# A two-layer attention and FFN kernel: the norm of batches 0 to 3 by itself, rings over the batches, sums held over, and the last token tile in two parts

## The reference

```
x = x + L0_xattn(norm(x), ctx)   # 16 heads of 32, causal over the first 100 context rows
x = x + L0_ffn(norm(x))          # 8 experts of 352, the best 2 per token, softmax over the two
x = x + L1_xattn(norm(x), ctx)   # 16 heads, see below
x = x + L1_ffn(norm(x))          # gated, 1408 wide; activations and weights rounded to 127 steps
```

## Time and profile before

| what | value |
|---|---|
| median of 3 runs | 829.26 us (828.37 to 829.54) |
| profiled execution | 826.05 us |
| its span | 824.0 us |
| granted TensorE clock, mean | 0.923 |
| instructions | 12030 |

### The profile page before, as it was taken

How to read it: one execution, slowest core, us unless ns; L and a number is a source line. 1 busy time by engine, 2 the same in 40 slices (tenths; PEclk the granted TensorE clock), 3 DMA queues, 4 the chain that set the end, 5 groups by cost and what they waited for, 6 DMA issues and landing times.

```text
span 824.0 us, 12030 instructions
## 1 busy us (share of the span) xinstructions
PE 688.8 (84%) x4235; PEld 550.3 (67%) x4235; DVE 511.2 (62%) x1038; ACT 416.0 (50%) x777; POOL 249.4 (30%) x278
## 2 busy tenths in 40 slices
PE   0799999654999999994688888988888799799985
PEld 0587777444777777694687777977777477566542
DVE  4886677474666656537647666367666544777674
ACT  3523567353555655421247767457676523455552
POOL 2000841332212322064008546128274001122232
PEclk9988999665999999995689999999999989999998
DMA  8565942599565565696100223212357982111000
GB/s 261 185 220 153 321 118 86 189 382 330 165 231 165 176 191 155 218 316 159 31 1 19 61 59 76 67 38 60 89 146 193 335 309 72 52 51 39 14 14 29
DMA packets 82972, 119.00 MB, mean 144 GB/s; under 512 B 40769, under 2 KB 63037, under 8 KB 79329
## 3 DMA queue, kind: packets, MB, share of 16 engines
q1 hardware_dynamic: 79777, 109.71, 41.4%
q0 software_dynamic: 3136, 8.53, 4.0%
HBM read 97.15 MB, written 27.62 MB: 151 GB/s over the span
## 4 chain that ended last, share of the span: by engine, by line
PE 55%; DVE 14%; issue 13%; ACT 8%; DMA 4%; POOL 2%; ACTq 1%; SPq 1%; another core or an unknown queue 0%; DVEq 0%; POOLq 0%
PE PS L149 12%; PE PS L151 11%; PE PS L150 10%; PE PS L1249 3%; PE PS L1425 3%; PE PS L1310 3%; PE PS L1609 2%; ACT w_hi L902 2%; DMA raw<-wkv_in 2%; DVE wscale L1867 1%; PE PS L1340 1%; POOL wraw L849 1%; PE PS L1351 1%; PE PS L1629 1%; DVE X L1972 1%
## 5 line engine op out<-in xcount | busy, mean ns | idle before, releaser
L849 POOL TENSOR_TENSOR wraw<-wraw,rinv 128x361 f32<-128x361 f32 (+1 forms) x104 | 80.6, 786 | 124.1 <-DVE rinv L1825 123.6
L1668 DVE TENSOR_TENSOR w_lo<-w,w_hi 128x1408 fp32r<-128x1408 f32 x40 | 64.8, 1620 | 40.3 <-ACT w_hi L902 40.3
L1832 DVE TENSOR_REDUCE nmx<-PS 128x1 f32<-128x361 f32 (+1 forms) x104 | 54.8, 527 | 36.4 <-PE PS L151 35.9
L991 ACT ACTIVATE wraw<-PS,nmx 128x361 f32<-128x361 f32 (+1 forms) x104 | 58.6, 565 | 31.9 <-DVE nmx L1832 18.2
L877 POOL TENSOR_TENSOR wraw<-gs,us 128x352 f32<-128x352 f32 (+1 forms) x28 | 26.7, 952 | 133.5 <-ACT gs L1165 106.3
L800 POOL DMA_INDIRECT xb<-xn_scratch,rows x20 | 35.1, 1756 | 103.7 <-PE PS L1221 100.6
L1835 DVE TENSOR_TENSOR pt_lo<-PS,pt_hi 128x384 fp32r<-128x384 f32 (+1 forms) x104 | 55.5, 534 | 16.4 <-ACT pt_hi L997 15.6
L902 ACT CAST w_hi<-w 128x1408 fp32r x40 | 54.7, 1369 | 18.8 <-issue 18.8
L149 PE MATMUL PS<-w_hi,xt_hi 128*128 128x352 f32 x160 | 57.1, 357 | 5.4 <-DVE xt_lo L1662 4.9
L1425 PE MATMUL PS<-ident,wraw 128*128 128x128 f32 x312 | 51.7, 275 | 11.6 <-DVE pt_lo L1835 5.5
L1249 PE MATMUL PS<-w,ht 128*128 128x512 f32 (+1 forms) x120 | 54.9, 593 | 0.6 <-DVE ht L1680 0.6
(11 more groups left out here) (270 smaller groups left out, 1872.6 us busy)
## 6 DMA issues: line engine op xcount, KB each, us to landing
w<-w_in SPq DMA_DIRECT2D x20, 768.0 KB, 5.8
w<-w_in SPq DMA_DIRECT2D x8, 1408.0 KB, 11.7
fq_raw<-foldq_in SPq DMA_DIRECT2D x6, 1088.0 KB, 7.5
cx_raw<-tile_scratch SPq DMA_DIRECT2D x6, 1024.0 KB, 4.9
ys_scratch<-yb SPq DMA_DIRECT2D x20, 256.0 KB, 5.7
ctx_scratch<-ctxo SPq DMA_DIRECT2D x24, 192.0 KB, 1.9
fp_raw<-foldp_in SPq DMA_DIRECT2D x6, 640.0 KB, 5.2
wraw<-wup_in SPq DMA_DIRECT2D x12, 256.0 KB, 4.4
```

What stands on the lines that cost most here:

```text
L849: pool.tensor_tensor(P1[slot][0:rows, 0:NK], P1[slot][0:rows, 0:NK], rinv[0:rows, jj, t:t + 1].broadcast_to((rows, NK)), ALU.mult).then_in ...
L991: act.activation(P1[t % 8][r, 0:NK], PS[r, t % 4, 0:NK], ACT.Exp, bias=nmx[r, jj, t:t + 1], accum_out=rsum[r, jj, t:t + 1]).then_inc(C["ex ...
L1668: dve.tensor_tensor(WL[which][:, :], w12_of(dve_wlo.e, which), WH[which][:, :].bitcast(F32), ALU.subtract) \
L1832: dve.tensor_reduce(nmx[r, jj, t:t + 1], PS[r, t % 4, 0:NK], AX.X, ALU.max, negate=True).then_inc(C["max"], 1)
```

## The change

- `lnc_vec` and its square root are split into two halves: `lnc_moments(h)`, `lnc_std(h)`, `lnc_rstd(h)` for batches 4h to 4h + 3. DVE's order becomes: folds 0 to 2, weigh 0, fold 3, weigh 1, fold 4, weigh 2 and 3, moments of half 0, fold 5, reciprocal of half 0, normalise 0 and 1, weigh 4, fold 6, weigh 5, fold 7, low halves of batches 0 to 3; weigh 6 and 7 stand behind queries 0 and 1, moments of half 1 behind query 1, its reciprocal and normalisations 4 and 5 behind query 2. ACT's square root of half 0 stands ahead of its copy of fold 6, that of half 1 ahead of its copy of query 3. PE turns batches 4 to 7 ahead of queries 4 to 7. The last gathered row block lies elsewhere.
- The rings for scores, turned weights and exponentials count row tiles over all batches (`row_tile` = 13 n + t). The keys take the bank that is due there.
- In the list, with 8 queries: PT 11 and 12 come at the last query's tick; PV parts that would be due later come there too; the fourth group's PV of the pair's second batch moves into the next pair, one part each at ticks 1, 2, 3. With 16 queries it stands at the last query's tick.
- Scores of an even batch's tiles 0 to 3 wait for the queries that they read and for the last one in their bank; an odd batch's wait for none; the keys are waited for at tile 0.
- The last token tile's rounding, subtraction and transposes go in two parts (7 and 4 column blocks), and `pe_down` waits for each group's copy where it needs it, in all tiles.

```diff
-KBANK = 4 + (KVAT - LAG) % 3
-        YG_PLACES = [YG_AT + 4 * D * i for i in range(15)] + [2 * FQB]
+        YG_PLACES = [YG_AT + 4 * D * i for i in range(15)] + [MOE_AT]
+        def lnc_moments(dve, h):
+            half = slice(h * B // 2, (h + 1) * B // 2)
+            seen = 2 * B + (h + 1) * B // 2
+            dve.wait_ge(LN["stats"], seen)
+            for b in range(half.start, half.stop):
+                dve.bn_aggr(mv[:, b, :], stats[:, b, :]).then_inc(LN["moments"], 1)
+            dve.wait_ge(LN["moments"], seen)
+            dve.tensor_scalar(veps[:, half], mv[:, half, 1], LN_EPS, None, ALU.add).then_inc(LN["var"], 1)
+        def lnc_std(act, h):
+            act.wait_ge(LN["var"], 3 + h)
+            act.activation(std[:, half], veps[:, half], ACT.Sqrt).then_inc(LN["std"], 1)
+        def lnc_rstd(dve, h):
+            dve.wait_ge(LN["std"], 3 + h)
+            dve.reciprocal(rstd[:, half], std[:, half]).then_inc(LN["rstd"], 1)
...
-        def pair_steps(last, vector, asked):
+        def pair_steps(last, vector, asked, held_over):
             ticks = [("S", b, t) for b in range(2) for t in range(RT)]
+            after = len(ticks)
             ticks += [("PR", 2, k) for k in asked] if not last else []
+            few = not last and len(asked) == SECOND
+            if held_over:
+                due += [(1 + c, 0, ("PV", -1, (NG - 1) * LK + c)) for c in range(LK)]
             for b in range(2):
                 for t in range(RT):
+                    at, order = RT * b + t + LAG, 1
+                    if at >= after:
+                        at = after + 2 * (at - after)
+                        if few and t >= RT - 2:
+                            at, order = after + SECOND - 1, 0 if t == RT - 2 else 2
+                    elif vector and at + 1 < after:
+                        at += 1
+                    due.append((at, order, ("PT", b, t)))
+                for g in range(NG - 1):
+                    for c in range(LK):
+                        at = RT * b + 3 * g + 2 + LAG
+                        at = (at if at < after else after + 2 * (at - after)) + PVLAG + c
+                        if few and at >= after + PVLAG + 1:
+                            at = after + SECOND - 1
+                        due.append((at, 1 if at == after + SECOND - 1 else 0, ("PV", b, g * LK + c)))
+                at = RT - 1 + LAG + PVLAG + 2 if b == 0 else after + len(asked) - 1 if not last else after + 2 * (LAG - 1) + PVLAG + 2
+                if b == 0 or not few:
+                    due += [(at, 0, ("PV", b, (NG - 1) * LK + c)) for c in range(LK)]
...
+        def scores_bank(n, t):
+            return row_tile(n, t) % 4
+        def turned_bank(n, t):
+            return 4 + row_tile(n, t) % 3
+        def weights_slot(n, t):
+            return row_tile(n, t) % 8
...
-                    wait(pe, C["exp"], RT * m + earlier(t, 4) + 1)
-                    if t < 4:
-                        pe.wait_ge(C["prl"], asked_at(m // 2, FIRST + SECOND - 1) + 1)
+                    wait(pe, C["exp"], row_tile(m, t) - 4 + 1)
+                    if m % 2 == 0 and t < 4:
+                        pe.wait_ge(C["prl"], asked_at(m // 2, max(last_query(t), last_in_bank(scores_bank(m, t)))) + 1)
+                    if t == 0:
                         wait(pe, C["ktl"], m + 1)
...
-            dve_fold(dve, 3, 3)
             weigh(0)
+            dve_fold(dve, 3, 3)
+            weigh(1)
             dve_fold(dve, 4, 0)
-            weigh(1)
+            weigh(2)
+            weigh(3)
+            lnc_moments(dve, 0)
             dve_fold(dve, 5, 1)
-            weigh(2)
-            dve_fold(dve, 6, 2)
-            weigh(3)
-            dve_fold(dve, 7, 3)
-            for b in range(4, B):
-                weigh(b)
-            lnc_vec(dve)
+            lnc_rstd(dve, 0)
             normalise(dve, 2, 0)
             normalise(dve, 2, 1)
+            weigh(4)
+            dve_fold(dve, 6, 2)
+            weigh(5)
+            dve_fold(dve, 7, 3)
...
+                if k < 2:
+                    weigh(6 + k)
+                if k == 1:
+                    lnc_moments(dve, 1)
+                if k == B // 2 - 2:
+                    lnc_rstd(dve, 1)
+                    normalise(dve, 2, B // 2)
+                    normalise(dve, 2, B // 2 + 1)
...
+        def hidden_parts(n):
+            return [slice(128 * a, 128 * z) for a, z in HTG] if n == NTT - 1 else [slice(0, FI)]
-                act.activation(H1[j][0:r, :], H1[j][0:r, :], ACT.Identity, bias=mgc[0:r, 0:1], scale=sh[0:r, j, 2:3]) \
-                    .then_inc(F["hmag"], 1)
+                for cols in hidden_parts(n):
+                    act.activation(H1[j][0:r, cols], H1[j][0:r, cols], ACT.Identity, bias=mgc[0:r, 0:1], scale=sh[0:r, j, 2:3]) \
+                        .then_inc(F["hmag"], 1)
```

146 lines of the change are left out of this document (77 added, 69 removed).

## The result

The changed kernel took 798.22 us (median of four runs, 796.05 to 803.56) beside 829.4 us for the kernel before (828.37 to 830.92): ratio 0.9632, 95% interval 0.958 to 0.9684, or 31.2 us less. The direction was right and the size too small. The profiled executions took 826.05 us before and 796.05 us after, spans 824.0 and 794.2 us: 29.8 us to be accounted for, stage by stage.

The account below looks back on a forecast made before the run. It took TensorE to bound nearly all of attention, VectorE ahead of it, and a chain of small steps at the end. Terms 9.0 + 6.0 + 1.5 + 5.2 + 1.7 + 0.7 = 24.1 us gave 805.2 us, range 799.5 to 815.

Parts of the forecast that it names:

- I put half of that, 0.36, down to the slots: Borders inside a pair: half of the 0.72 us late context copy blamed on exponential slots, giving 1.74 per border.
- I take 1.5 each: Four borders inside a pair: 1.74 us each lowered to 1.5, since ScalarE and GpSimd lose their catch-up pause.
- Added: ... 1.1: Borders 1 to 2 and 5 to 6: new waits at query 14 and the first held sum, 1.1 off 4.0 us.
- Norm of batches 0 to 3: Ahead of attention: splitting off this norm starts queries near 392.3 instead of 402.8; 9.0 us left, bounds 5 and 10.5.
- land 5.5 us after issue: Gathers ahead of the norm: batch 3's rows, issued at 365.20, would land about 371.7, in time for weighing 3.
- Rings: Four borders inside a pair: banks and slots counted on remove waits at tile 0; 6.0 us, ends 4 and 7.2.
- Borders between pairs: Batches 1 to 2 and 5 to 6: 5.2 us for both; batches 3 to 4: 1.7 us, hiding splitting.
- First queries to batch 0: First scores wait for the split of query 12 rather than 15: 1.5 us, ends 0.8 and 1.7.
- The last tile: 32-token tile at the end: rounding and subtraction in two parts start the down projection earlier; 0.7 us, ends 0.2 and 1.3.
- the rule of the Trainium skill that I had set aside: Last tile: by the VectorE and GpSimd port lock the gain would be 0.4 us; dismissed as changing nothing above.
- the rivals: Slow queries 811 (0.17); inside-pair releaser changes 812.7 (0.08); between-pair edits fail 813.6 (0.06); lower attention clock 836.3 (0.03).
- The slower one: Attention: with fewer pauses the chip grants a lower clock; 836.3 us at 70 us of it; chance 0.03.

Follow-up runs that it names:

- Session 1: First measurement of the change: changed kernel 798.22 us beside 829.4 us for the kernel before, ratio 0.9632.
- session 5: Kernel before 820.4 us, its copy 820.01; changed kernel 796.69, with the norm of all eight batches together 798.67; kernel before with only VectorE's order changed 819.07.
- session 4: Kernel before 827.7 us, changed kernel 795.62; changed kernel plus early table load 796.5, plus unread products among the queries 796.66, plus both and further covers 799.55.
- session 2: Kernel before 819.8 us, changed kernel 796.73; changed kernel with one part undone: norm 799.31, ring counting 803.51, step list 801.69.
- session 6: Kernel before 828.6 us, its copy 828.84; changed kernel with the norm of all eight batches together again 811.45, ratio 0.9772.

## Why the prediction was right and wrong

The time came out 1.3 us below the range. The mechanism of every part was seen where the forecast put it; what failed are sizes, above all three steps that held the sum down: "I put half of that, 0.36, down to the slots" with "I take 1.5 each" (rings: 6.0 forecast, 8.24 measured), "Added: ... 1.1" (nothing of it to be seen), and the drops of the clock that had rows and no term (at the last projection 4.88 us, and at the output projection), put at nothing. The norm was sized too high, and that hid part of it.

**What bounds the kernel** was read rightly: the gains came from TensorE's idle time and its clock.

**Norm of batches 0 to 3.** Forecast 9.0 us at the start of the queries' work, and 1.5 at the first border; together 10.5 at the first exponential. Session 1 gave 8.2. The queries started at 395.54, not 392.3: VectorE came to fold 5's low half at 384.16 instead of 379.06, because its first weighing waited 3.75 us for the gathered rows and it stood 2.08 and 1.47 us with no releaser before the next two steps; from there it took 11.4 us to the first query product instead of the 13.2 forecast.
A reading that failed, though little hung on it, is "land 5.5 us after issue". That row is the median of only the landings that the trace has, and of the 16 it has two, those of the last two gathers. Beside it the kernel before in session 5, where all 16 are there, and the changed kernel in session 4, where none is:

```profile
yg<-ys_scratch,slots POOLq DMA_INDIRECT x16, 9.4
...
yg<-ys_scratch,slots POOLq DMA_INDIRECT x16
```

In the twelve traces that have all landings the eighth gather takes 9.2 to 13.4 us, so by them the rows of batch 3 land at an estimated 374.4 or later and not at 371.7. In session 2 the changed kernel's fourth weighing waits 0.31 us for them; the first one waits 4.06 us for its own, and fold 5 still comes 30.3 us behind E (30.8 in the forecast's base).
What the forecast did not see either is that its base was itself a disturbed execution. In the sessions with the kernel before at 820 the fold products end 27.8 us after E in ten traces of twelve (32 in two), and in the three sessions with it at 828 or 829 in none of eight: 34.7 to 41.9 us. I call the first sessions quiet and the others disturbed. With the old order, E to Q goes from 48.5 to 50.6 us (quiet) up to 54.6 to 60.2 (disturbed), and with the new one from 42.2 to 45.0 only up to 43.4 to 46.5. In the disturbed traces the first query product comes 18.3 to 20.0 us behind the last fold product in the old order, with four weighings and the whole norm in between, and 6.2 to 8.6 us in the new one.
So the idle 5.09 us ahead of fold 5 belong to that execution: the kernel before in session 5 has no wait there, and the first query still comes 6.3 to 7.9 us earlier with the new norm in the quiet sessions, with two weighings (2.17 us each) and half of the norm behind it instead of ahead and TensorE's first transposes ahead of weighings 4 and 5. Of the total this is 2.0 to 2.6 us in a quiet session, not clear of the scatter, and by the ratios (0.9772 in session 6 against 0.9632 and 0.9644 in 1 and 4, across sessions and chips) 10.6 to 11.6 us in a disturbed one. How that divides between the filled gap and the halves is not shown.
The Trainium skill's price of a table switch (ScalarE: Activation LUTs, "What ACT_TABLE_LOAD costs") adds a drain of about 1.38 us to the load. The traces do not show it at the other switch either; of the old-norm version in session 2:

```profile
424.05 0.89 ACT L1028 CAST q_hi<-PS 128x400 fp32r<-128x400 f32 x2 [0.38 <-PE PS L1443]
424.96 1.28 ACT L1052 ACT_TABLE_LOAD   x1
426.25 0.56 ACT L1052 ACTIVATE wraw<-PS,nmx 128x361 f32<-128x361 f32 x1
```

The copies end at 424.94, the load starts at 424.96, and the exponential follows it at once, at 426.25.

**Rings: forecast 6.0, measured 8.24** in session 2 (the bound was 7.2). The mechanism is as forecast; the step that failed is "I put half of that, 0.36, down to the slots" and then "I take 1.5 each". By its size the whole of the 0.72 us behind the late exponential came back: 1.38 + 0.72 = 2.10 of stake against 2.06 of gain. Banks and slots were not undone separately. GpSimd did not become late: transposes wait 2.8 us in all for its scaled weights, and 3.6 before.

**Borders between pairs: forecast 5.2 + 1.7.** Border 3 to 4 gave 0.8 for the list and 1.0 for the wait, 1.8. Borders 1 to 2 and 5 to 6 gave 3.7 and 3.8 in session 1 after the rings' share (2.06) is taken out: 2.3 for the list, measured by itself, and 1.4 to 1.5 for the drop of the clock. At stake were 4.0, and the step that failed is "Added: ... 1.1": the new list added nothing that can be seen. The held sum starts with no wait, where 0.5 was forecast, and query 14 waits 0.37 instead of 0.6. The clock's part was forecast as sure, and it is not: of six traces with the old borders (the kernel before, its copies and its two versions) five have that drop at border 1 to 2 and two at 5 to 6; those of the changed kernel have none, nor do the two with the old list or the one with the old rings alone. Which part of the change keeps it away is thus open.

**First queries to batch 0: forecast 1.5.** The wait is gone, but ScalarE's table load (1.28 us) now stands straight ahead of the first exponential, which moved early gave 0.4 us, and the norm's new work among the queries takes back the rest: Q to X is the same (29.72 and 29.73). With the old norm and the new wait it is 26.9 to 28.2, and 28.2 to 29.7 in the kernel before, so a gain of about 1.5 is there by itself. Behind it lay a drop of the clock in batch 0, 0.7 us, which I had a row for (0.67 against 0.40 us) and did not cost.

**The last tile: forecast 0.7, measured 2.2.** The parts give 0.42 in session 1. The projection gives 2.33 by its clock, a term that stood in the rows as 4.88 us and that I left out, and 0.52 of it went at once: the drop of the clock came one tile earlier (779.6 to 783.2) and the rounding later. It is so wherever the last projection ran at 1.00 without fillers, in four of twelve traces with the parts: there L to the rounding takes 11.18 to 11.53 us, in all others 10.77 to 10.86. In the other eight the projection ran at 0.50 to 0.63 (3.90 to 4.85 us; 4.22 for the changed kernel in sessions 2 and 4), and in the six traces without parts and fillers at 0.50 to 0.60. So most of the 1.8 us is where the drop fell in that execution, and that the parts move it is not shown.
Here the rule of the Trainium skill that I had set aside decides (SBUF — State Buffer, "Who interferes with whom"): the shared port pair is locked for a whole instruction, and whoever issues first has it. The last tile of the old-norm version of session 2:

```profile
786.99 2.00 DVE L2147 TENSOR_SCALAR wraw<-wraw 32x896 bf16<-32x896 f32 x2
787.15 1.56 POOL L944 TENSOR_TENSOR x_tiles<-x_tiles,y 128x512 f32<-128x512 f32 x1 [2.64 <-DVE y L2153]
```

GpSimd's add is 1.26 us where it starts alone and 1.56 where VectorE's first part was ahead of it; the second part then ends 2.00 us after the first began, 0.28 behind the add's end. Undivided, the subtraction ends 0.75 us behind the end of the add before the change and 0.74 in the old tail, wherever the add began. The undivided one takes 1.31 us beside the add. All these fit a full block and not a slowing. By the page the gain was an estimated 0.4, and 0.42 is what session 1 shows; in that there is luck, since the parts give 0.10 to 0.54 us in the twelve traces, depending on when the add starts.

**Not foreseen: 1.9 us at the output projection.** In session 1 its start was at granted clock 0.57 before and 1.00 after. P to G is 24.3 to 25.8 us in the traces of the kernel before, 23.4 to 24.8 in four of the changed one and 23.9 to 26.0 in its versions. All six traces with the old attention have a stretch at the lower clock there, and so have nine of the fourteen others: mostly scatter of the clock, and whether the change has a share in it was not tested.

**The sum.** Norm and first border -2.3 against the forecast, rings and borders up to the last exponential +5.3 (18.2 against 12.9), the last tile +1.5, projection +1.9 and +0.1, and -0.8 for experts that ended later: 24.1 + 5.7 = 29.8. Some 7 us of the 29.8 are clock (3.0 at the two borders, 0.7 in batch 0, 1.9 and 1.8 behind), and the forecast had 3.4 of them. In the quiet sessions 2 and 5 the change is worth 23 to 24 us, which is near the 24.1 by luck, through another sum (of the stages of session 5: -6.3, +1.6, -16.8, -0.8, -0.4, -1.2, -2.2, which is 26.1 in the two traces where the medians are 23.7 apart).
Of the rivals none came. The slower one, a lower clock under denser attention, is excluded by the granted 1.00 all through it.

**What stays open.** What disturbs the gather stretch: sessions 2, 4 and 5 ran on one chip, and 4 alone was disturbed, so it is not the chip. The gathers are issued at the same times after E in all traces, the last one 27.3 to 28.4 us behind it. But the eight disturbed traces lack records: they hold 7321 to 7386 semaphore events in all, the twelve others 7621 to 7627, the missing ones lie in this stretch, and of the 16 landings 0 to 4 are there. So "issue" and "remote" in it can mean that the record of the releaser is missing, and whether the recording itself slows the stretch, or only suffers with it, no run here can tell. The order of VectorE without the halves was run in a quiet session only. The kernel before loses 8 to 9 us in a disturbed session, and its traces show 6 to 8 of them between E and Q; but the two pairs of traces of sessions 1 and 5 are 29.8 and 26.1 us apart, so of the 7.5 us between the gains of the medians (31.2 and 23.7) they place only 3.7.

## What to carry to other kernels

A profile of before is one execution: a wait with no releaser in it ("issue", "remote") may be a disturbance or a lost record, and a median time to landing may rest on two landings of sixteen. Look at both before a term is built on them. An order that puts less work behind the step that comes late is worth more in the sessions when it does come late. Cost a drop of the clock as its own term, with its own chance, wherever a dense stretch follows a pause, at the very end too; and do not expect a saved drop to show in the total, because it may come somewhere later. Where a wait and a late engine lie on one chain, as the 1.38 and 0.72 us at the rings, count both in full unless a row shows who is next.

## What the runs showed of the hardware

- Idle time with no releaser on TensorE (0.3 to 2.7 us) and on ScalarE ("remote", up to 5.1 us) in the stretch in which the sixteen gathers run, with late fold products in all eight traces of three sessions and in two of twelve of the others. In the eight, 240 to 300 semaphore events are missing from the record.
- The same program has the drop of the clock to 0.50 in one execution and not in the next, at the same place: 33.45 against 35.01 us at border 5 to 6.
- Products that only keep TensorE busy raised the clock where they stood (2.3 us in the last projection, 1.9 in the queries), and the time of the whole fell by 3.5 us in one case, with an interval that just reaches no change, and not at all in two.
- A drop of the clock that is gone from one place can be found at another: in the four traces with the last projection at 1.00 and no fillers, 0.3 to 0.7 us were lost ahead of the rounding.
- VectorE's subtraction on 32 rows of 1408 ends 0.75 us behind the end of GpSimd's add when it was issued during it (1.24 to 1.32 us long), and GpSimd's add takes 1.56 to 1.58 us instead of 1.26 when VectorE's first part was ahead of it.
